# Attention over a 64-word vocabulary: exponentials of four of sixteen heads with the maximum as a per-partition bias and the sums from the same instruction

## Chip, cores and metric

One core of a Trainium2 chip runs the whole program. The metric is the device time of one execution in microseconds (us), as the median of several runs. Engines are TensorE (PE, matmuls; PEld is its weight load), VectorE (DVE), ScalarE (ACT), GpSimd (POOL) and SyncE (SP, which issues DMAs). All data are float32.

## The reference, cut to what matters

The program is a small language-model tower: token attention, a recurrent layer, and an expert layer. The change lies in the token attention. There are 32 sequences of 128 tokens from a vocabulary of 64 words, 16 heads of 16 dimensions:

```
emb = emb_W.T[input_seq] + emb_b
q, k, v = emb @ Wq.T + bq, emb @ Wk.T + bk, emb @ Wv.T + bv     # per head
scores = einsum('bqhd,bkhd->bhqk', q, k) / sqrt(d)
probs = softmax(scores, axis=-1)
ctx = einsum('bhqk,bkhd->bqhd', probs, v)
y = ctx @ Wo.T + bo + emb            # then a normalisation over each sequence
```

A token's row depends only on its word and on how often each word occurs in its sequence. So the kernel computes, for each sequence, the 64 rows of its words and not 128 rows of tokens: the score of a query word and a key word, plus the logarithm of the key word's count in the sequence, goes into the softmax over 64 key words.

## The kernel before, in words

Two sequences lie on the 128 partitions at a time (64 query words each), which makes 16 pairs. `score` [128, 16 heads, 64 keys] is computed once; `logc` holds the logarithms of the counts, one row of 64 per pair. The function `token_attention` has a first block that makes these tables, and a second block, with the change in it, that goes over the pairs. The steps for one pair, with their lines, are:

- GpSimd `logits`, L401: logit = score + logc, 1024 elements a partition. It waits for the exponential of two pairs earlier (buffers are double).
- VectorE `softmax_input`: L430 takes the maximum of each head into `ps_top`, which lies in PSUM; L431 subtracts it from `logit` in place, 16 heads at once.
- ScalarE `exponential`, L476: one Exp over 1024 elements into `prob`.
- GpSimd `partial_sums`: L409 adds the two halves of each head's 64 probabilities (512 results), and L411 the halves of that (256 results), waiting for L409 by a semaphore.
- VectorE `denominators`: L438 sums the remaining 16 of each head, L439 takes the reciprocal.
- TensorE `transpose_prob`, L518: eight transposes into PSUM; ScalarE `copy_prob`, L482, copies them to SBUF; TensorE `context`, L526, multiplies by the values.
- ScalarE `repeat_inverse`, L488, TensorE `spread`, L536, and ScalarE `copy_spread`, L493, bring the reciprocals into the layout of the context.
- VectorE `normalise`, L446, multiplies both into `cx_t`; TensorE `project`, L544; VectorE `output`: L453 adds the embedding, L455 takes statistics, L456 copies six numbers a partition into `stats6`, SBUF to SBUF. ScalarE `keep_row`, L497, stores the row.

Each engine works through its own list in a fixed order. In the turn of pair n the order is:

```
POOL: logits(n), partial_sums(n-1)
DVE:  softmax_input(n), normalise(n-2), denominators(n-1), output(n-3)
ACT:  copy_prob(n-1), copy_spread(n-2), exponential(n), repeat_inverse(n-1), keep_row(n-3)
PE:   context(n-1), project(n-2), transpose_prob(n), spread(n-1)
```

The first four and the last three turns are written out with the missing pairs left out, and the twelve turns between run in a hardware loop of two turns each. The recurrence and the expert layer follow, each in blocks of its own, behind a barrier.

Of the kernel before, what the change touches and what calls it, by code (L numbers as in the profile page):

```python
# [13 lines left out]
F32 = mybir.dt.float32  # L14
I32 = mybir.dt.int32
ALU = mybir.AluOpType
ACT = mybir.ActivationFunctionType
AX = mybir.AxisListType

P = 128  # L20
B, T = 32, 128
E, C = 256, 64
H, D = 16, 16
# [11 lines left out]
START = 16  # L35


class Chain:
# [15 lines left out]
    def enter(self, i, per, first=0):  # L54

        self.base, self.k, self.i, self.per, self.first = self.base + self.k, 0, i, per, first
# [102 lines left out]
def token_attention(nc, a, m, sem, sb):  # L159
# [177 lines left out]
    with ExitStack() as ctx:  # L337
        def sbx(n, s):
            return ctx.enter_context(nc.sbuf_tensor(n, s, F32))
        logit = [sbx(f"logit{i}", [P, H, C]) for i in range(2)]  # L340
        prob = [sbx(f"prob{i}", [P, H * C]) for i in range(2)]
        prob_t = [sbx(f"prob_t{i}", [P, HP, P]) for i in range(2)]
        half = [sbx(f"half{i}", [P, H, C // 2]) for i in range(2)]
        quarter = [sbx(f"quarter{i}", [P, H, C // 4]) for i in range(2)]
        den = [sbx(f"den_h{i}", [P, H]) for i in range(2)]
        rden = [sbx(f"rden_h{i}", [P, H]) for i in range(2)]
        r_rep = [sbx(f"r_rep{i}", [P, H, D]) for i in range(2)]
# [4 lines left out]
        ps_t = ctx.enter_context(nc.psum_tensor("ps_t", [P, HP * P], F32))  # L352
        ps_c = [ctx.enter_context(nc.psum_tensor(f"ps_c{i}", [P, 512], F32)) for i in range(2)]
        ps_y = [ctx.enter_context(nc.psum_tensor(f"ps_y{i}", [P, 512], F32)) for i in range(2)]
        ps_top = ctx.enter_context(nc.psum_tensor("ps_top", [P, 512], F32))
        block = ctx.enter_context(nc.Block())

        def par(name):
            return [sem(f"{name}{i}") for i in range(2)]
        sc_ok, lg_ok, ex_ok, hf_ok, dn_ok, rd_ok, rr_ok, rs_mm, rs_ok = (  # L360
            par(n) for n in ("sc_ok", "lg_ok", "ex_ok", "hf_ok", "dn_ok", "rden_ok", "rr_ok", "rs_mm", "rs_ok"))
        pt_mm, pt_ok, cx_mm, cx_ok, y_mm, y_ok, h_ok = (
            par(n) for n in ("pt_mm", "pt_ok", "cx_mm", "cx_ok", "y_mm", "y_ok", "h_ok"))
        TURNS = PAIRS // 2

        def pairs(t, s, live):

            for back in range(4):
                yield (t - (back + 1 - s) // 2, (s + back) % 2) if back in live else None

        def turns(work, enter=None):

            for n in range(4):
                work(*pairs(n // 2, n % 2, range(0, n + 1)))
            yield
            for n in range(1, 4):
                work(*pairs(TURNS + (n - 1) // 2, (n - 1) % 2, range(n, 4)))

        def run(eng, work, enter=None, leave=None):

            prefix = turns(work)
            next(prefix)
            with eng.Fori(2, TURNS) as t:
                if enter:
                    enter(t)
                for s in range(2):
                    work(*pairs(t, s, range(4)))
            if leave:
                leave()
            for _ in prefix:  # L390
                pass
# [5 lines left out]
        @block.gpsimd  # L397
        def _(pool):
            def logits(i, s):
                pool.wait_ge(ex_ok[s], START + i)  # L400
                nc.gpsimd.tensor_tensor(logit[s][:], score[:],  # L401
                                        logc[:, bass.ds(2 * i + s, 1)].broadcast_to([P, H, C]), ALU.add)\
                    .then_inc(sc_ok[s], 1)

            def partial_sums(i, s):
                p = prob[s][:].rearrange("p (h c) -> p h c", c=C)
                pool.wait_ge(ex_ok[s], START + i + 1)
                pool.wait_ge(rd_ok[s], START + i)
                nc.gpsimd.tensor_tensor(half[s][:], p[:, :, 0:C // 2], p[:, :, C // 2:], ALU.add).then_inc(hf_ok[s], 1)  # L409
                pool.wait_ge(hf_ok[s], START + i + 1)  # L410
                nc.gpsimd.tensor_tensor(quarter[s][:], half[s][:, :, 0:C // 4], half[s][:, :, C // 4:], ALU.add)\  # L411
                    .then_inc(dn_ok[s], 1)

            def work(p0, p1, p2, p3):
                if p0:
                    logits(*p0)
                if p1:
                    partial_sums(*p1)

            run(nc.gpsimd, work)  # L420

        @block.vector
        def _(dve):
            ch = Chain(dve, sem("v_chain1"))

            def softmax_input(i, s):

                top = ps_top[:, s * H:(s + 1) * H]
                dve.wait_ge(sc_ok[s], START + i + 1)
                ch.link(nc.vector.reduce_max(top, logit[s][:], AX.X))  # L430
                nc.vector.tensor_tensor(logit[s][:], logit[s][:], top.unsqueeze(2).broadcast_to([P, H, C]),  # L431
                                        ALU.subtract).then_inc(lg_ok[s], 1)

            def denominators(i, s):

                dve.wait_ge(dn_ok[s], START + i + 1)
                dve.wait_ge(rr_ok[s], START + i)
                ch.link(nc.vector.reduce_sum(den[s][:], quarter[s][:], AX.X))  # L438
                nc.vector.reciprocal(rden[s][:], den[s][:]).then_inc(rd_ok[s], 1)  # L439

            def normalise(i, s):

                dve.wait_ge(cx_mm[s], START + i + 1)
                dve.wait_ge(rs_ok[s], START + i + 1)
                dve.wait_ge(y_mm[s], START + i)
                nc.vector.tensor_tensor(cx_t[s][:].rearrange("p k c -> p (k c)"), ps_c[s][:, 0:E],  # L446
                                        r_sp[s][:].rearrange("p k c -> p (k c)"), ALU.mult).then_inc(cx_ok[s], 1)

            def output(i, s):

                dve.wait_ge(y_mm[s], START + i + 1)
                dve.wait_ge(h_ok[s], START + i)
                nc.vector.tensor_tensor(yrow[s][:], ps_y[s][:, 0:E], base[:], ALU.add).then_inc(y_ok[s], 1)  # L453
                dve.wait_ge(y_ok[s], START + i + 1)
                ch.link(nc.vector.bn_stats(bn[s][:], yrow[s][:]))  # L455
                nc.vector.tensor_copy(stats6[:, bass.ds(2 * i + s, 1)], bn[s][:].unsqueeze(1))  # L456

            def work(p0, p1, p2, p3):
                if p0:
                    softmax_input(*p0)  # L460
                if p2:
                    normalise(*p2)
                if p1:
                    denominators(*p1)
                if p3:
                    output(*p3)

            run(nc.vector, work, lambda t: ch.enter(t, 6, 2), lambda: ch.leave(TURNS))

        @block.scalar  # L470
        def _(act):
            def exponential(i, s):
                act.wait_ge(lg_ok[s], START + i + 1)
                act.wait_ge(pt_mm[s], START + i)
                act.wait_ge(hf_ok[s], START + i)
                nc.scalar.activation(prob[s][:], logit[s][:].rearrange("p h c -> p (h c)"),  # L476
                                     ACT.Exp).then_inc(ex_ok[s], 1)

            def copy_prob(i, s):
                act.wait_ge(pt_mm[s], START + i + 1)  # L480
                act.wait_ge(cx_mm[s], START + i)
                nc.scalar.copy(prob_t[s][:].rearrange("p g c -> p (g c)"), ps_t[:]).then_inc(pt_ok[s], 1)  # L482

            def repeat_inverse(i, s):

                act.wait_ge(rd_ok[s], START + i + 1)
                act.wait_ge(rs_mm[s], START + i)
                nc.scalar.copy(r_rep[s][:], rden[s][:].unsqueeze(2).broadcast_to([P, H, D])).then_inc(rr_ok[s], 1)  # L488

            def copy_spread(i, s):  # L490
                act.wait_ge(rs_mm[s], START + i + 1)
                act.wait_ge(cx_ok[s], START + i)
                nc.scalar.copy(r_sp[s][:].rearrange("p k c -> p (k c)"), ps_c[s][:, E:2 * E]).then_inc(rs_ok[s], 1)  # L493

            def keep_row(i, s):
                act.wait_ge(y_ok[s], START + i + 1)
                nc.scalar.copy(h_tab[:, bass.ds(2 * i + s, 1)], yrow[s][:].unsqueeze(1)).then_inc(h_ok[s], 1)  # L497

            def work(p0, p1, p2, p3):
                if p1:  # L500
                    copy_prob(*p1)
                if p2:
                    copy_spread(*p2)
                if p0:
                    exponential(*p0)
                if p1:
                    repeat_inverse(*p1)
                if p3:
                    keep_row(*p3)

            run(nc.scalar, work)
# [1220 lines left out]
```

## Time and profile before

| | us |
|---|---|
| median of 3 runs | 904.01 |
| lowest and highest | 898.59, 905.11 |
| the profiled execution, device time | 905.7 |
| its span, first to last instruction | 904.0 |
| TensorE clock granted, mean, as a share of full | 0.902 |
| the block of the 16 pairs, within the span | about 30.5 to 119 |

The page gives, over the whole span, TensorE busy 719.5 us (80%), VectorE 615.3 (68%), ScalarE 355.3 (39%) and GpSimd 452.9 (50%). These shares mix stages that have different limits, so that the block of the 16 pairs has to be read by itself. A timeline row gives the start, the length and the idle time before an instruction. Lines of the kernel are given as L401, and so on. Instructions on one engine overlap a little in these rows: the next may start up to 0.1 us before the one ahead has ended.

### The profile page before, as it was taken

How to read it: one execution, taken by the hardware profiler on the slowest of the kernel's cores; microseconds unless marked ns; L12 is line 12 of the kernel's file. 1: busy time of each engine (PE TensorE's matmuls, PEld its weight loads, DVE VectorE, ACT ScalarE, POOL GpSimd, SP SyncE). 2: the span in 40 equal slices, each digit the busy share in tenths (PEclk: the TensorE clock that was granted, in tenths of full speed). 3: DMA queues.
4: the chain of work that ended last, by engine and by line, in shares of the span. 5: the costliest groups of instructions: out<-in, count | busy, mean ns of one | idle time of the engine just before them, and what ended most of it. 6: DMA issues, size and time to landing. Idle time of an engine off the chain costs nothing. (4 is left out here: it accounts for less than half of the span.)

```text
span 904.0 us, 20491 instructions
## 1 busy us (share of the span) xinstructions
PE 719.5 (80%) x7708; PEld 484.6 (54%) x7708; DVE 615.3 (68%) x913; ACT 355.3 (39%) x562; POOL 452.9 (50%) x257
## 2 busy tenths in 40 slices
PE   3566758895999999999999999986899679867644
PEld 2354534443777777777777777755676423322221
DVE  1688847777899999999999999983676501100004
ACT  2456523442544545455454545433456221010100
POOL 1588700000799999999999999991221000000000
PEclk9789869987899999999999999996999879877875
DMA  4000010000001010000000000004900579999936
GB/s 107 1 1 0 0 49 0 0 0 14 6 12 34 13 36 12 12 12 12 12 9 9 12 12 12 14 13 152 348 26 2 208 282 410 417 416 416 402 121 209
DMA packets 48892, 86.34 MB, mean 96 GB/s; under 512 B 5233, under 2 KB 32433, under 8 KB 48849
## 3 DMA queue, kind: packets, MB, share of 16 engines
q1 hardware_dynamic: 43248, 81.23, 24.3%
q10 hardware_dynamic: 5600, 4.53, 1.6%
q8 instruction: 28, 0.46, 0.2%
q14 instruction: 16, 0.12, 0.0%
HBM read 76.31 MB, written 9.44 MB: 95 GB/s over the span
## 5 line engine op out<-in xcount | busy, mean ns | idle before, releaser
L859 POOL TENSOR_TENSOR read<-state,q_pos 128x1024 f32<-128x1024 f32 x128 | 300.4, 2366 | 28.0 <-DVE state L968 21.7
L968 DVE TENSOR_TENSOR_SCAN state<-fac,ps_up 128x1024 f32<-128x1024 f32 x128 | 290.0, 2277 | 13.0 <-ACT fac L903 12.6
L903 ACT ACTIVATE fac<-ps_xf 128x1016 f32<-128x1016 f32 x128 | 130.3, 1018 | 174.7 <-PE ps_xf L998 163.7
L998 PE MATMUL ps_xf<-hot,xtab 64*128 64x128 f32 x2048 | 149.0, 285 | 9.9 <-ACT fac L903 9.9
L998 PEld LDWEIGHTS ps_xf<-hot,xtab 64*128 64x128 f32 x2048 | 126.3, 189 | 56.4 <-ACT fac L903 45.2
L998 PE MATMUL ps_up<-hot,utab 64*128 64x128 f32 x2048 | 140.7, 277 | 18.2 <-DVE state L968 16.8
L998 PEld LDWEIGHTS ps_up<-hot,utab 64*128 64x128 f32 x2048 | 127.1, 190 | 23.7 <-issue 16.0
L868 POOL TENSOR_TENSOR utab<-tab 128x1024 f32 (+1 forms) x32 | 64.5, 2014 | 106.5 <-SPq L85 106.5
L1041 PE MATMUL ps_o<-read,sel 128*32 128x256 f32 x1024 | 82.7, 395 | 3.7 <-POOL read L859 3.7
L1582 DVE COPY h_t<-ps_ht 128x512 f32<-128x512 f32 x16 | 10.4, 687 | 78.1 <-PE ps_ht L1610 78.1
L958 DVE TENSOR_TENSOR xtab<-tab,ps_k 128x1024 f32<-128x1024 f32 x64 | 59.5, 929 | 1.5 <-PE ps_k L990 1.5
L1622 PE MATMUL ps<-w_sb,h_t 128*32 128x256 f32 x512 | 37.6, 448 | 19.1 <-DMA w_sb<-in_L_ffn_w 19.1
L401 POOL TENSOR_TENSOR logit<-score,logc 128x1024 f32<-128x1024 f32 x16 | 37.8, 2362 | 24.7 <-SPq L85 24.7
L1600 PE MATMUL ps<-w_sb,mq 128*32 128x512 f32 x256 | 40.8, 781 | 6.3 <-DMA w_sb<-in_L_ffn_w 6.3
L753 PE MATMUL ps_qk<-w_all,x_t 128*128 128x512 f32 x64 | 35.6, 685 | 7.5 <-ACT x_t L700 7.5
L1584 DVE COPY eo<-ps 128x256 f32 x8 | 3.4, 425 | 56.0 <-PE ps L1622 56.0
L958 DVE TENSOR_TENSOR utab<-tab,ps_k 128x1024 f32<-128x1024 f32 x32 | 38.3, 1196 | 0.0
L1521 ACT COPY mq<-merged 128x256 f32 (+1 forms) x8 | 3.2, 404 | 88.4 <-PE ps L1622 87.7
L1622 PEld LDWEIGHTS ps<-w_sb,h_t 128*32 128x32 f32 x512 | 17.5, 124 | 36.8 <-issue 24.8
L1376 PE MATMUL pq_h<-w_out,y_t 128*128 128x256 f32 x128 | 31.1, 386 | 5.9 <-DVE y_t L1299 5.9
L920 ACT COPY xtab<-xtab 128x512 f32<-128x512 f32 x32 | 34.8, 1088 | 0.0
L1041 PEld LDWEIGHTS ps_o<-read,sel 128*32 128x32 f32 x1024 | 20.2, 108 | 23.8 <-POOL read L859 5.5
(203 smaller groups left out, 979.6 us busy)
## 6 DMA issues: line engine op xcount, KB each, us to landing
w_sb<-in_L_ffn_w SPq DMA_DIRECT2D x32, 2048.0 KB, 19.5
rec_out<-osb SPq DMA_DIRECT2D x128, 32.0 KB, 1.5
ao<-rec_out SPq DMA_DIRECT2D x8, 512.0 KB, 4.0
out_dram<-res ACTq DMA_DIRECT2D x8, 512.0 KB, 2.8
tok<-in_x SPq DMA_DIRECT2D x2, 512.0 KB, 7.6
exp_out<-eo SPq DMA_DIRECT2D x8, 128.0 KB
oq<-exp_out SPq DMA_DIRECT2D x2, 512.0 KB, 4.2
w_nat<-in_L_tok_Wq SPq DMA_DIRECT2D x1, 256.0 KB, 9.0
```

What stands on the lines that cost most here:

```text
L401: nc.gpsimd.tensor_tensor(logit[s][:], score[:], logc[:, bass.ds(2 * i + s, 1)].broadcast_to([P, H, C]), ALU.add)\
L753: last = nc.tensor.matmul(ps_qk[s][:], x1_t[s][:, k], w_all[:, k, 0:2 * E], start=k == 0, stop=k == KT - 1)
L859: nc.gpsimd.tensor_tensor(read[n % 2][:], state[n % 4][:].rearrange("p (b i t) -> p b i t", b=2, i=IB), q_pos[x.s][:, :, x.k].unsqueeze(2) ...
L868: nc.gpsimd.tensor_tensor(out, feat, k_feat.rearrange("p (h j) -> p h j", j=D).unsqueeze(1) .broadcast_to([P, D // 2, HB, D]), ALU.mult).t ...
L903: nc.scalar.activation(fac[n % 2][:].rearrange("p (n t) -> p n t", t=T)[:, :, 1:], ps_x[:].rearrange("p (n t) -> p n t", t=T)[:, :, 1:], A ...
L920: nc.scalar.copy(rows[:, D // 2:, :, 0:D // 2], rows[:, 0:D // 2, :, D // 2:].rearrange("p j h i -> p i h j")).then_inc(t_act, 1)
L958: nc.vector.tensor_tensor(out[:, :, :, cols], feat[:, :, :, cols], ps_k[:, x.k * P:(x.k + 1) * P].rearrange("p (h j) -> p h j", j=D)[:, :, ...
L968: nc.vector.tensor_tensor_scan(state[n % 4][:], fac[n % 2][:], ps_u[n % 2][:], 0.0, ALU.mult, ALU.add)\
L998: last = nc.tensor.matmul(dst[:, b * 512 + col * T:b * 512 + (col + 1) * T], stationary[rows], pos[rows], start=True, stop=True)
L1041: last = nc.tensor.matmul(ps_o[32 * ii:32 * ii + 32, x.k * 256:(x.k + 1) * 256], sel[:, x.block], read[n % 2][:, :, ii], start=x.block == ...
L1600: last = nc.tensor.matmul(ps_1[s][j * B:(j + 1) * B, cols], mq[s][:, k, j], w1[s][:, j, k, cols], start=False, stop=k == KT - 1, skip_grou ...
L1622: last = nc.tensor.matmul(ps_2[s][j * B:(j + 1) * B, 0:E], h_t[:, n, j * B:(j + 1) * B], w2[s][:, j, n], start=False, stop=n == HT - 1, sk ...
```

## The change

For the last four heads VectorE no longer subtracts the maximum. The reduction (with `negate`) writes the negated maxima of all sixteen heads into a tile `low` in SBUF, and has a semaphore `mx_ok` of its own. VectorE then adds `low` to the logits of the first twelve heads. For each of the last four heads ScalarE runs an Exp of 64 elements with that head's column of `low` as the bias and with `accum_out`, which puts the sum into the head's column of `den`. Then it takes the Exp of the first twelve heads, 768 elements, as before. GpSimd's partial sums and VectorE's last sum are over twelve heads. The PSUM tile `ps_top` is gone. ScalarE's four small instructions wait for `mx_ok`, and for the transposes and the reciprocals of two pairs earlier; the large one waits for `lg_ok` and `hf_ok`.

```diff
--- before.py
+++ after.py
@@ -340,8 +340,10 @@
         logit = [sbx(f"logit{i}", [P, H, C]) for i in range(2)]
         prob = [sbx(f"prob{i}", [P, H * C]) for i in range(2)]
         prob_t = [sbx(f"prob_t{i}", [P, HP, P]) for i in range(2)]
-        half = [sbx(f"half{i}", [P, H, C // 2]) for i in range(2)]
-        quarter = [sbx(f"quarter{i}", [P, H, C // 4]) for i in range(2)]
+        HV = H - 4
+        half = [sbx(f"half{i}", [P, HV, C // 2]) for i in range(2)]
+        quarter = [sbx(f"quarter{i}", [P, HV, C // 4]) for i in range(2)]
+        low = [sbx(f"low{i}", [P, H]) for i in range(2)]
         den = [sbx(f"den_h{i}", [P, H]) for i in range(2)]
         rden = [sbx(f"rden_h{i}", [P, H]) for i in range(2)]
         r_rep = [sbx(f"r_rep{i}", [P, H, D]) for i in range(2)]
@@ -352,13 +354,12 @@
         ps_t = ctx.enter_context(nc.psum_tensor("ps_t", [P, HP * P], F32))
         ps_c = [ctx.enter_context(nc.psum_tensor(f"ps_c{i}", [P, 512], F32)) for i in range(2)]
         ps_y = [ctx.enter_context(nc.psum_tensor(f"ps_y{i}", [P, 512], F32)) for i in range(2)]
-        ps_top = ctx.enter_context(nc.psum_tensor("ps_top", [P, 512], F32))
         block = ctx.enter_context(nc.Block())
 
         def par(name):
             return [sem(f"{name}{i}") for i in range(2)]
-        sc_ok, lg_ok, ex_ok, hf_ok, dn_ok, rd_ok, rr_ok, rs_mm, rs_ok = (
-            par(n) for n in ("sc_ok", "lg_ok", "ex_ok", "hf_ok", "dn_ok", "rden_ok", "rr_ok", "rs_mm", "rs_ok"))
+        sc_ok, mx_ok, lg_ok, ex_ok, hf_ok, dn_ok, rd_ok, rr_ok, rs_mm, rs_ok = (
+            par(n) for n in ("sc_ok", "mx_ok", "lg_ok", "ex_ok", "hf_ok", "dn_ok", "rden_ok", "rr_ok", "rs_mm", "rs_ok"))
         pt_mm, pt_ok, cx_mm, cx_ok, y_mm, y_ok, h_ok = (
             par(n) for n in ("pt_mm", "pt_ok", "cx_mm", "cx_ok", "y_mm", "y_ok", "h_ok"))
         TURNS = PAIRS // 2
@@ -403,7 +404,7 @@
                     .then_inc(sc_ok[s], 1)
 
             def partial_sums(i, s):
-                p = prob[s][:].rearrange("p (h c) -> p h c", c=C)
+                p = prob[s][:].rearrange("p (h c) -> p h c", c=C)[:, 0:HV]
                 pool.wait_ge(ex_ok[s], START + i + 1)
                 pool.wait_ge(rd_ok[s], START + i)
                 nc.gpsimd.tensor_tensor(half[s][:], p[:, :, 0:C // 2], p[:, :, C // 2:], ALU.add).then_inc(hf_ok[s], 1)
@@ -425,17 +426,18 @@
 
             def softmax_input(i, s):
 
-                top = ps_top[:, s * H:(s + 1) * H]
                 dve.wait_ge(sc_ok[s], START + i + 1)
-                ch.link(nc.vector.reduce_max(top, logit[s][:], AX.X))
-                nc.vector.tensor_tensor(logit[s][:], logit[s][:], top.unsqueeze(2).broadcast_to([P, H, C]),
-                                        ALU.subtract).then_inc(lg_ok[s], 1)
+                nc.vector.tensor_reduce(low[s][:], logit[s][:], AX.X, ALU.max, negate=True).then_inc(mx_ok[s], 1)
+                dve.wait_ge(mx_ok[s], START + i + 1)
+                nc.vector.tensor_tensor(logit[s][:, 0:HV], logit[s][:, 0:HV],
+                                        low[s][:, 0:HV].unsqueeze(2).broadcast_to([P, HV, C]),
+                                        ALU.add).then_inc(lg_ok[s], 1)
 
             def denominators(i, s):
 
                 dve.wait_ge(dn_ok[s], START + i + 1)
                 dve.wait_ge(rr_ok[s], START + i)
-                ch.link(nc.vector.reduce_sum(den[s][:], quarter[s][:], AX.X))
+                ch.link(nc.vector.reduce_sum(den[s][:, 0:HV], quarter[s][:], AX.X))
                 nc.vector.reciprocal(rden[s][:], den[s][:]).then_inc(rd_ok[s], 1)
 
             def normalise(i, s):
@@ -465,15 +467,20 @@
                 if p3:
                     output(*p3)
 
-            run(nc.vector, work, lambda t: ch.enter(t, 6, 2), lambda: ch.leave(TURNS))
+            run(nc.vector, work, lambda t: ch.enter(t, 4, 2), lambda: ch.leave(TURNS))
 
         @block.scalar
         def _(act):
             def exponential(i, s):
+                act.wait_ge(mx_ok[s], START + i + 1)
+                act.wait_ge(pt_mm[s], START + i)
+                act.wait_ge(rd_ok[s], START + i)
+                for h in range(HV, H):
+                    nc.scalar.activation(prob[s][:, h * C:(h + 1) * C], logit[s][:, h], ACT.Exp, bias=low[s][:, h:h + 1],
+                                         scale=1.0, accum_out=den[s][:, h:h + 1])
                 act.wait_ge(lg_ok[s], START + i + 1)
-                act.wait_ge(pt_mm[s], START + i)
                 act.wait_ge(hf_ok[s], START + i)
-                nc.scalar.activation(prob[s][:], logit[s][:].rearrange("p h c -> p (h c)"),
+                nc.scalar.activation(prob[s][:, 0:HV * C], logit[s][:, 0:HV].rearrange("p h c -> p (h c)"),
                                      ACT.Exp).then_inc(ex_ok[s], 1)
 
             def copy_prob(i, s):

```

## Rows read from the trace of the kernel before

**Rows 1.** Windows view: busy us of PE, PEld, DVE, ACT, POOL; clock; DMA share, GB/s.

```profile
...
30.00:48.00 18.00, 9.75 (x64) 7.57 (x64) 11.38 (x13) 7.27 (x10) 15.91 (x11) 0.62 0.00 1
63.00:68.00 5.00, 3.97 (x26) 3.19 (x14) 4.71 (x9) 1.75 (x3) 4.49 (x4) 0.66 0.00 0
30.00:119.40 89.40, 57.10 (x480) 43.54 (x480) 72.60 (x128) 49.87 (x82) 69.29 (x48) 0.85 0.00 0
```

**Rows 2.** Groups by line and shape, 40 to 110 us: total, mean ns, idle before.

```profile
...
L401 POOL TENSOR_TENSOR logit<-score,logc 128x1024 f32<-128x1024 f32 x14 | 33.1, 2365 | 0.0
...
L409 POOL TENSOR_TENSOR half<-prob 128x512 f32<-128x512 f32 x14 | 17.9, 1277 | 7.6 <-ACT prob L476 7.6
...
L431 DVE TENSOR_TENSOR logit<-logit,ps_top 128x1024 f32<-128x1024 f32 x14 | 17.1, 1221 | 0.5
L430 DVE TENSOR_REDUCE ps_top<-logit 128x16 f32<-128x1024 f32 x14 | 17.1, 1219 | 2.2 <-POOL logit L401 1.9
...
L411 POOL TENSOR_TENSOR quarter<-half 128x256 f32<-128x256 f32 x14 | 10.3, 736 | 1.1
...
L438 DVE TENSOR_REDUCE den_h<-quarter 128x16 f32<-128x256 f32 x13 | 5.3, 408 | 0.0
```

**Rows 3.** Timeline, a pair at the full clock: start us, length us, instruction, idle before.

```profile
...
88.27 1.22 DVE L431 TENSOR_TENSOR logit<-logit,ps_top 128x1024 f32<-128x1024 f32 x1
...
89.52 1.06 ACT L476 ACTIVATE prob<-logit 128x1024 f32<-128x1024 f32 x1 [1.17 <-DVE logit L431]
...
89.88 1.13 PE L544 MATMUL ps_y<-w_t,cx_t 128*128 128x256 f32 x4 [1.10 <-DVE cx_t L446]
...
90.74 1.28 POOL L409 TENSOR_TENSOR half<-prob 128x512 f32<-128x512 f32 x1 [0.52 <-ACT prob L476]
...
90.84 1.04 PE L518 MATMUL ps_t<-ident,prob 128*128 128x128 f32 x8
...
91.34 0.70 DVE L456 COPY stats<-bn 128x6 f32 x1 [0.16 <-DVE bn L455]
...
91.96 1.22 DVE L430 TENSOR_REDUCE ps_top<-logit 128x16 f32<-128x1024 f32 x1
91.99 1.01 ACT L482 COPY prob_t<-ps_t 128x1024 f32<-128x1024 f32 x1 [0.72 <-PE ps_t L518]
```

**Rows 4.** Timeline, a pair at the lower clock.

```profile
...
64.29 2.01 PE L544 MATMUL ps_y<-w_t,cx_t 128*128 128x256 f32 x4 [1.03 <-DVE cx_t L446]
...
66.10 1.87 PE L518 MATMUL ps_t<-ident,prob 128*128 128x128 f32 x8
...
68.01 1.01 ACT L482 COPY prob_t<-ps_t 128x1024 f32<-128x1024 f32 x1 [2.32 <-PE ps_t L518]
...
69.18 1.07 ACT L476 ACTIVATE prob<-logit 128x1024 f32<-128x1024 f32 x1
```

**Rows 5.** Timeline, the copy of L456 after GpSimd's last instruction.

```profile
...
115.70 0.17 DVE L456 COPY stats<-bn 128x6 f32<-128x6 f32 x1
```

**Rows 6.** Instructions of L1222, min/median/max ns, in the expert gate's softmax.

```profile
...
L1222 ACT ACTIVATE pr<-lg_q,nmx x8: 401/403/403, 648.2 to 723.5; 128x128 f32<-128x128 f32 x8
L1222 ACT ACTIVATION_READ_ACCUMULATOR pr<-lg_q,nmx x8: 186/188/191, 648.5 to 723.8; 128x1 f32 x8
```

**Rows 7.** VectorE with two SBUF operands, 24 to 29 us.

```profile
...
L289 DVE TENSOR_TENSOR log_diag<-ident,cnt 128x1024 f32<-128x1024 f32 x1 | 1.2, 1224 | 0.0
...
L294 DVE TENSOR_TENSOR v_pair<-v_tab,row_half 128x256 f32<-128x256 f32 x1 | 0.4, 426 | 0.0
```

**Rows 8.** Timeline of GpSimd, 29 to 34 us.

```profile
...
30.48 4.64 POOL L401 TENSOR_TENSOR logit<-score,logc 128x1024 f32<-128x1024 f32 x2 [24.69 <-SPq L85]
```

**Rows 9.** Timeline of ScalarE: its exponentials of pairs 0, 3 and 15.

```profile
...
35.37 1.06 ACT L476 ACTIVATE prob<-logit 128x1024 f32<-128x1024 f32 x1 [2.79 <-DVE logit L431]
...
49.15 1.07 ACT L476 ACTIVATE prob<-logit 128x1024 f32<-128x1024 f32 x1
...
109.78 1.07 ACT L476 ACTIVATE prob<-logit 128x1024 f32<-128x1024 f32 x1
```


## Prediction, on record before the change was run

> **What bounds the kernel now.** I read the windows of the block first, then its groups by shape, then the timeline of one pair at each level of the clock. In the windows the reader is to see that no DMA runs in these 89.4 us, that VectorE is busy 72.6 and GpSimd 69.3 of them, and that TensorE's clock falls from full to 0.66 in single pairs and to 0.62 in the filling [rows 1]. The block is a tenth of the span, and nothing behind its barrier reads what the change touches except through its end, so whatever the change does is a shift of that end. The exponentials of pairs 3 and 15 start at 49.15 and 109.78 [rows 9]: 60.63 us for twelve pairs, 5.05 each. That is the number to move.
>
> Two rings share that period. At the full clock VectorE's own list is the ring: the subtraction starts at 88.27, and the next can start when the maximum of 91.96 has ended, at about 93.2, so 4.94 us [rows 3]. ScalarE waits 1.17 us for VectorE there. At the lower clock it is TensorE and ScalarE: the projection takes 2.01 instead of 1.13 us and the transposes 1.87 instead of 1.04, the copy of the probabilities starts at 68.01, and the exponential follows at 69.18 with no wait for VectorE [rows 3, 4].
>
> One row in VectorE's list is more than its work. The copy of six numbers, L456, takes 0.17 us once GpSimd has finished [rows 5], but 0.70 us beside GpSimd's L409: it ends at 92.04, L409 at 92.02 [rows 3]. It is held until GpSimd's instruction ends, then needs 0.02 us, and VectorE's next maximum waits behind it. The subtraction L431 keeps its 1.22 us beside the 2.37 us additions of GpSimd; its second operand is in PSUM [rows 2].
>
> **The change part by part.**
>
> *VectorE.* An element costs (1221-426)/768 = 1.035 ns, with L431 for the 1024 and a 256-element addition in SBUF for the other end [rows 2, 7]. So 768 elements take 0.95 us, 0.27 less. The last sum, L438 with 408 ns for 256, loses 64 elements: 0.07 less. The maximum into SBUF instead of PSUM I cost at nothing (a VectorE addition of 1024 takes 1224 ns into SBUF and L430 1219 into PSUM [rows 2, 7]; bound 0 to 0.05). Its new semaphore wait replaces the one of the chain. In all 0.34 us less in a list of 4.9.
>
> *GpSimd.* (1277-736)/256 = 2.11 ns an element [rows 2]: L409 falls by 0.27 to 1.01 us, L411 by 0.14 to 0.60. The additions L401 stay at 2.37. GpSimd's list falls from 4.38 to 3.98 us a pair.
>
> *ScalarE.* The large exponential falls from 1.06 to about 0.85 us. Four small ones are added. The nearest row is L1222, bias, sum and 128 elements: 403 ns, with a second instruction of 188 ns that reads the accumulator [rows 6]. With 64 fewer elements at 0.83 ns that is 0.35 plus 0.19; neighbours overlap by up to 0.09, once or twice, so 0.35 to 0.44 each after the first overlap. I take 0.40, so 1.6 us for the four, bounds 1.4 and 1.8. Net +1.4 us of ScalarE a pair. At the full clock ScalarE has 1.17 us of wait ahead of the exponential [rows 3] and the small ones need only the maximum, so most of it hides there: they run while VectorE subtracts. At the lower clock there is no wait, and all 1.4 us lies on the ring. Queued behind the four are the large exponential, the repeat of the inverses and the row's copy; who waits is TensorE's transposes and GpSimd's L409. (The Trainium skill, "ScalarE: Activation LUTs", section "What ACT_TABLE_LOAD costs", gives 280 ns plus 0.833 ns an element with a bias pointer: an estimate of 0.33 us for 64 elements, and for 128 it gives 387 where the trace has 403; with it the four would take about 1.7 us.)
>
> ScalarE's ring after the change: 1.17 from the copy's start to the exponential's [rows 4], 1.6, 0.85 less 0.1, 0.1 to TensorE, the transposes 1.04 or 1.87 [rows 3, 4], and 0.1 to the next copy (90.84+1.04 to 91.99 [rows 3]): 4.8 us at the full clock, 5.65 at the lower.
>
> *The place of the maxima.* The subtraction now has both operands in SBUF. No row shows such an instruction beside a running GpSimd instruction: the two of rows 7 ran before 29 us, and GpSimd sat idle until 30.48 [rows 7, 8]. The nearest rows point both ways: L431 with a PSUM operand is not held, the copy L456 is. So the bounds are no wait at all and the whole of an L401, 2.37 us. The sum L438, which reads one SBUF tile and writes another, keeps its 408 ns and is free too [rows 2], so it is not enough that nothing is in PSUM. I take it, as the likelier half, that two SBUF operands are held like the copy; the instruction then pays only its streaming, 0.80 us, after the release. (The Trainium skill, "SBUF — State Buffer", section "Who interferes with whom", says so outright: a VectorE instruction with two SBUF inputs contends with a GpSimd instruction that reads SBUF, and the second to issue is blocked until the first has finished. It speaks against this change. The trace agrees as to the copy; as to two inputs no row shows it. By it rival 2 below falls away.)
>
> **What the period becomes.** If held, VectorE's subtraction and GpSimd's three instructions share one way. Where the subtraction goes in ahead of the next L401, the ring is 2.37 + 1.01 + 0.08 + 0.60 + 0.80 and 0.02 for the copy = 4.9 us, about ScalarE's 4.8. From pair 3 on, with four of the twelve pairs at the lower clock as now (the window from 63 us, and three like it from 73, 94 and 104 [rows 1]): 8 x 4.9 + 4 x 5.65 = 61.8, against 60.63: +1.2 us. The filling, at 0.62 of the clock, goes from 13.78 us between exponentials 0 and 3 [rows 9] to three rounds of 5.65 less the part for which the clock is up again, about 16.3: +2.5. The first subtraction, which ended just ahead of the exponential of 35.37 and so began at about 34.1 [rows 9], would be held by the second L401, which ends at 35.12 [rows 8]: +0.6. Sum +4.3 us on a span of 904.0 and a device time of 905.7, so a profile of 910.0; from the median 904.0 it is 908.3. Bounds of the four exponentials move it by 1.5 to 2.5: 904 to 912.
>
> **The rivals.**
>
> 1. *Held, and GpSimd goes first (slower).* When L411 ends, L401 is queued right behind it, and the subtraction waits too. No row tells who is let through. If it is GpSimd, or if VectorE comes after L401 has begun, the subtraction sits out all of L401, and the exponential, L409 and L411 come behind it one after another: exponential 0.89, 0.16 to GpSimd (90.58 to 90.74 [rows 3]), 1.01, 0.08, 0.60, 2.37, then 0.80 = 5.9 us. VectorE's next maximum only starts when the copy is released at the end of L409, and so comes too late again: the state keeps itself up. It decides where the maximum ends later than L411, that is 0.7 us after L409. Twelve pairs give 70.8: +10.2, with the filling +13.3, so 917; lower-clock pairs may add 0.9 each, up to 921. For it: the copy's 0.70 us. Against: VectorE would have been waiting longer.
>
> 2. *Not held.* VectorE's ring falls to 4.6 us and ScalarE's of 4.8 and 5.65 sets the period: 61.0 for twelve, +0.4, with +2.5 in the filling: 907. For it: L431 and L438 run undisturbed beside GpSimd [rows 2]. It gives nearly the same time as the forecast; the rows of the subtraction tell them apart.
>
> 3. *The small exponentials all hide.* ScalarE is busy 49.9 of 89.4 us [rows 1]. If lower-clock pairs get rare, 12 x 4.7 = 56.4: -4.2, about 900. Against: the ring above, which has no slack.
>
> **How the numbers follow.** Forecast (held, subtraction ahead of L401) 0.38, rival 1 0.36, rival 2 0.18, rival 3 0.05, anything else 0.03. The likeliest time is 908.3, its own range 904 to 912. For 8 in 10 the range has to take in most of rival 1: 903 to 919. One per cent, 9 us, is about what a measurement of this kernel can tell. Over it lies nearly all of rival 1 and a little of the forecast's upper end: slower 0.39; faster 0.02; the rest 0.59.
>
> **What the profile would show.** Subtraction rows at 0.95 us beside GpSimd: not held. Rows of 1 to 3 us that end some 0.02 to 0.8 us behind the end of a GpSimd instruction: held; if they end behind L401, rival 1, and GpSimd then waits for ScalarE before each L409. Four exponentials of 0.35 us with four reads of 0.19. ScalarE's wait for VectorE gone at the full clock, TensorE's transposes waiting for `prob`. L409 near 1.01 and L411 near 0.60. Everything behind the block shifted as a whole. The prediction is wrong if the later blocks change length, if the small exponentials cost over 0.5 us each, or if the clock's level changes over the block.

## The result and the profile after

| | before | after |
|---|---|---|
| median, 17 runs each | 902.32 us | 914.26 us |
| lowest and highest | 898.01, 905.53 | 905.63, 918.46 |
| ratio, 95% interval | | 1.0124 [1.0105, 1.0143] |
| profiled execution: device time, span | 905.7, 904.0 | 913.17, 911.4 |
| block of the 16 pairs, first L401 (L402) to the next block's table load | 30.48 to 119.37 | 28.53 to 129.46 |

The change makes the kernel 1.24% slower, 11.9 us by the medians. In the profiled executions the block lasts 88.9 us before and 100.9 after, 12.0 more. The rest of the program took 4.6 us less in the profiled execution of after (1.95 ahead of the block, the others behind it), which is why the span grew by 7.4 only; runs of one kernel differ by as much.

From here on the lines are those of the changed kernel: L402 is the large addition (L401 before), L410 and L412 the partial sums (L409, L411), L430 the maximum, L432 the subtraction (L431), L458 the copy of the six numbers (L456), L479 the small exponentials and L483 the large one (L476). The windows view of after, with the columns of [rows 1]:

```profile
...
104.00:109.00 5.00, 4.33 (x22) 3.44 (x26) 4.71 (x7) 2.48 (x6) 3.90 (x3) 0.50 0.00 0
28.50:129.00 100.50, 63.12 (x480) 46.91 (x480) 82.63 (x127) 66.62 (x209) 65.84 (x48) 0.78 0.00 0
```

VectorE is busier by 10 us than in [rows 1], though it was given less to do, GpSimd has 3.5 us less, and TensorE has the same 480 matmuls at a mean clock of 0.78 instead of 0.85. The groups by shape, from 40 to 125 us, with total, mean ns and idle before, answer to [rows 2], which go from 40 to 110:

```profile
...
L402 POOL TENSOR_TENSOR logit<-score,logc 128x1024 f32<-128x1024 f32 x13 | 31.3, 2410 | 0.0
L432 DVE TENSOR_TENSOR logit<-logit,low 128x768 f32<-128x768 f32 x14 | 27.5, 1966 | 0.5
...
L479 ACT ACTIVATE prob<-logit,low 128x64 f32<-128x64 f32 x56 | 18.8, 345 | 0.0
...
L410 POOL TENSOR_TENSOR half<-prob 128x384 f32<-128x384 f32 x15 | 15.0, 1000 | 25.8 <-ACT prob L483 25.8
...
L412 POOL TENSOR_TENSOR quarter<-half 128x192 f32<-128x192 f32 x15 | 11.0, 731 | 1.2
L479 ACT ACTIVATION_READ_ACCUMULATOR prob<-logit,low 128x1 f32 x56 | 10.9, 195 | 0.0
```

The subtraction of 768 elements has a mean of 1966 ns where 1024 elements took 1221 [rows 2]. GpSimd's first sum costs 1.00 us, as worked out, but GpSimd sat idle ahead of it, waiting for the exponential, for 25.8 us in 15 sums, 1.7 each; in [rows 2] it was 7.6 in 14, 0.5 each. The small exponentials cost 345 and 195 ns. The next timeline shows how such a wait begins; each row is start, length, instruction, idle before:

```profile
...
56.23 1.00 POOL L410 TENSOR_TENSOR half<-prob 128x384 f32<-128x384 f32 x1
56.36 0.89 DVE L458 COPY stats<-bn 128x6 f32 x1 [0.20 <-DVE bn L457]
...
57.17 1.21 DVE L430 TENSOR_REDUCE low<-logit 128x16 f32<-128x1024 f32 x1
57.31 0.60 POOL L412 TENSOR_TENSOR quarter<-half 128x192 f32<-128x192 f32 x1
57.86 2.35 POOL L402 TENSOR_TENSOR logit<-score,logc 128x1024 f32<-128x1024 f32 x1
...
58.41 2.62 DVE L432 TENSOR_TENSOR logit<-logit,low 128x768 f32<-128x768 f32 x1
58.41 0.35 ACT L479 ACTIVATE prob<-logit,low 128x64 f32<-128x64 f32 x1
...
61.06 0.84 ACT L483 ACTIVATE prob<-logit 128x768 f32<-128x768 f32 x1 [1.22 <-DVE logit L432]
...
62.06 1.00 POOL L410 TENSOR_TENSOR half<-prob 128x384 f32<-128x384 f32 x1 [1.85 <-ACT prob L483]
```

GpSimd's first sum L410 starts at 56.23. The copy L458 is asked for at 56.36 and ends at 57.25, 0.02 us after L410. So the maximum starts only at 57.17 and the subtraction is asked for at 58.41, 0.55 us after the large addition L402 has begun. It runs to 61.03, which is 0.82 us after L402 has ended at 60.21: it was held for as long as the addition ran and then streamed its 768 elements. Everything behind it is late: the large exponential starts at 61.06, and GpSimd does nothing from 60.21 to 62.06. Nine subtractions in a row (pairs 5 to 13) take 2.23 to 2.63 us in this manner. The tenth escapes:

```profile
...
110.20 0.83 ACT L483 ACTIVATE prob<-logit 128x768 f32<-128x768 f32 x1
...
111.03 0.17 DVE L458 COPY stats<-bn 128x6 f32 x1 [0.16 <-DVE bn L457]
...
111.50 1.22 DVE L430 TENSOR_REDUCE low<-logit 128x16 f32<-128x1024 f32 x1 [0.30 <-issue]
...
112.26 0.59 POOL L412 TENSOR_TENSOR quarter<-half 128x192 f32<-128x192 f32 x1
112.75 0.96 DVE L432 TENSOR_TENSOR logit<-logit,low 128x768 f32<-128x768 f32 x1
112.82 3.10 POOL L402 TENSOR_TENSOR logit<-score,logc 128x1024 f32<-128x1024 f32 x1
```

Here the exponential is late for another reason (TensorE's lower clock, 0.50 in the window from 104 to 109 us above), GpSimd starts L410 late at 111.19, and the copy has slipped in ahead of it. The subtraction is asked for at 112.75, 0.07 us before the large addition is. It takes 0.96 us, and now the addition is the one that is held: 3.10 us instead of 2.35.

The starts of the large exponential give one pair of numbers for each kernel, the filling (pair 0 to 3) and twelve pairs (3 to 15), as in [rows 9]. They stand in this table for all runs, each from its profiled execution, beside the median and the ratio to the kernel before on the same chip, which had medians of 902.32 to 902.80 us:

| kernel | filling | twelve pairs | median us | ratio, 95% interval |
|---|---|---|---|---|
| before | 13.78 | 60.63 | | |
| after | 16.45 | 70.18 | 914.26 | 1.0124 [1.0105, 1.0143] |
| place_only | 14.57 | 65.15 | 909.62 | 1.0074 [1.0049, 1.0100] |
| place_stats_psum | 14.58 | 65.13 | 909.44 | 1.0089 [1.0057, 1.0121] |
| two_places | 15.70 | 55.68 | 900.83 | 0.9979 [0.9957, 1.0001] |
| after_stats_psum | 16.43 | 55.85 | 900.75 | 0.9957 [0.9928, 0.9985], without two of the six runs (see there) |
| before_stats_psum | 13.89 | 57.82 | 899.36 | 0.9961 [0.9941, 0.9982] |
| ordered | 16.42 | 60.41 | 904.21 | 1.0017 [0.9998, 1.0035] |
| two_stats_psum | 16.43 | 55.67 | 900.60 | 0.9980 [0.9958, 1.0001] |
| two_stats_hv2 | 14.55 | 56.52 | 901.19 | 0.9981 [0.9962, 1.0000] |
| two_hv8 | 19.16 | 70.01 | 919.05 | 1.0176 [1.0143, 1.0209] |
| no_accum | 15.38 | 60.01 | 902.60 | 1.0001 [0.9984, 1.0018] |

### The profile page after: what moved, and what is told of

The parts are those of the page before. It is cut to its first block and busy times, and to the rows that moved or that the text cites. A ratio compares the mean times of both kernels' runs of the same rounds, so it can differ in the third digit from the quotient of the medians.

```text
span 911.4 us, 20625 instructions
## 1 busy us (share of the span) xinstructions
PE 720.2 (79%) x7708; PEld 485.1 (53%) x7708; DVE 625.5 (69%) x913; ACT 371.8 (41%) x690; POOL 449.5 (49%) x257
## 5 line engine op out<-in xcount | busy, mean ns | idle before, releaser
L402 POOL TENSOR_TENSOR logit<-score,logc 128x1024 f32<-128x1024 f32 x16 | 38.3, 2397 | 22.8 <-SPq L85 22.8
L760 PE MATMUL ps_qk<-w_all,x_t 128*128 128x512 f32 x64 | 33.1, 643 | 9.2 <-ACT x_t L707 9.2
L551 PE MATMUL ps_y<-w_t,cx_t 128*128 128x256 f32 x64 | 23.8, 508 | 13.8 <-DVE cx_t L448 13.6
```

What stands on the lines that cost most here:

```text
L402: nc.gpsimd.tensor_tensor(logit[s][:], score[:], logc[:, bass.ds(2 * i + s, 1)].broadcast_to([P, H, C]), ALU.add)\
L760: last = nc.tensor.matmul(ps_qk[s][:], x1_t[s][:, k], w_all[:, k, 0:2 * E], start=k == 0, stop=k == KT - 1)
```

## The experiments

The theory after the result was: the subtraction's second operand in SBUF makes it and GpSimd's instructions exclude each other; whichever is asked for first goes first; the held copy brings VectorE late, and from then on each pair loses the overlap. The rival was that the small exponentials on ScalarE cost the time.

**place_only.** The kernel before with only the place of the maxima changed, sixteen heads and no small exponentials.

```diff
-                top = ps_top[:, s * H:(s + 1) * H]
+                top = low[s][:]
```

> The kernel before with one edit: the maxima go to a tile in SBUF instead of PSUM, sixteen heads as before, no small exponentials. Theory (the place of the maxima costs the time, the subtraction is held while GpSimd runs): subtraction rows of 2.5 to 3 us that end about 1.07 us after a GpSimd addition of 2.37; a ring of 1.06 + 0.16 + 1.28 + 0.08 + 0.74 + 2.33 + 1.07 = 6.7 us against 5.05, so up to 20 us slower than the kernel before, at least 8 if the subtraction often gets in ahead. Rival (the small exponentials cost the time): within 2 us of the kernel before.

Measured: 0.74% slower, with a period of 5.42 to 5.44 us in every pair from pair 2 on. Its timeline (L409, L411 and L401 are GpSimd's three, as before):

```profile
...
68.57 1.27 POOL L409 TENSOR_TENSOR half<-prob 128x512 f32<-128x512 f32 x1
68.65 1.22 DVE L430 TENSOR_REDUCE low<-logit 128x16 f32<-128x1024 f32 x1
...
69.91 1.23 DVE L431 TENSOR_TENSOR logit<-logit,low 128x1024 f32<-128x1024 f32 x1
69.92 1.81 POOL L411 TENSOR_TENSOR quarter<-half 128x256 f32<-128x256 f32 x1
...
71.69 2.36 POOL L401 TENSOR_TENSOR logit<-score,logc 128x1024 f32<-128x1024 f32 x1
...
74.01 1.27 POOL L409 TENSOR_TENSOR half<-prob 128x512 f32<-128x512 f32 x1
```

The subtraction is asked for at 69.91, L411 at 69.92. The subtraction takes its plain 1.23 us, and L411 takes 1.81 instead of 0.74: this time GpSimd is held. So the place alone costs 0.7% with no small exponential in the program, which the rival doesn't give. The size of 20 us was wrong, since from pair 2 on VectorE asks first each time, if only by 0.01 to 0.03 us; the milder figure of at least 8 was still above the 6.8 us measured. The period is the sum of what now excludes each other: 2.36 + 1.27 + 1.81 less overlaps of a few hundredths.

**place_stats_psum.** The same, and the statistics tile in PSUM.

```diff
-        bn = [sbx(f"bn{i}", [P, 6]) for i in range(2)]
+        bn = [ps_bn[:, 64 + 8 * i:64 + 8 * i + 6] for i in range(2)]
```

> The kernel before with the maxima in SBUF and the statistics tile in PSUM. Theory (in place_only the shared way itself is the ring: addition 2.36, first sum 1.27, subtraction 1.07, second sum 0.74, 5.43 us, with the subtraction already ahead of the addition): freeing the copy brings nothing, 5 to 8 us slower than the kernel before. Rival (the held copy costs in this kernel too): within 3 us of the kernel before.

Measured: 65.13 us for twelve pairs against 65.15, and 0.89% slower than before. The copy falls from 0.69 to 0.17 us and the period stays. Where VectorE asks first anyway, the held copy costs nothing that can be measured.

**two_places.** The changed kernel, its maxima in two reductions: those for ScalarE's bias in SBUF, those for the subtraction in PSUM.

```diff
-                nc.vector.tensor_reduce(low[s][:], logit[s][:], ...).then_inc(mx_ok[s], 1)
-                dve.wait_ge(mx_ok[s], START + i + 1)
+                nc.vector.tensor_reduce(low[s][:, HV:H], logit[s][:, HV:H], ...).then_inc(mx_ok[s], 1)
+                top = ps_top[:, s * H:s * H + HV]
+                ch.link(nc.vector.tensor_reduce(top, logit[s][:, 0:HV], ...))
...
-                                        low[s][:, 0:HV].unsqueeze(2).broadcast_to([P, HV, C]),
+                                        top.unsqueeze(2).broadcast_to([P, HV, C]),
```

> The changed kernel with the maxima in two reductions: those of the last four heads into SBUF for ScalarE, those of the twelve others into PSUM for the subtraction; the small exponentials with their sums stay. Theory (place): subtraction rows of 0.95 us throughout, GpSimd's first partial sum no longer late by 1.8 us, time between 1 us faster and 4 us slower than the kernel before. Rival (the small exponentials): still 8 to 12 us slower.

Measured: 900.83, a ratio of 0.9979, so by the two ratios 1.4% below the changed kernel with all of ScalarE's new work kept. The rival falls. One pair of its timeline (L434 is the subtraction, L481 the small exponentials, L485 the large one, L527 the transposes, L491 the copy of the probabilities):

```profile
...
65.06 1.01 ACT L491 COPY prob_t<-ps_t 128x1024 f32<-128x1024 f32 x1 [0.61 <-PE ps_t L527]
...
65.58 2.37 POOL L403 TENSOR_TENSOR logit<-score,logc 128x1024 f32<-128x1024 f32 x1
...
66.19 0.95 DVE L434 TENSOR_TENSOR logit<-logit,ps_top 128x768 f32<-128x768 f32 x1
66.23 0.36 ACT L481 ACTIVATE prob<-logit,low 128x64 f32<-128x64 f32 x1
...
67.56 0.83 ACT L485 ACTIVATE prob<-logit 128x768 f32<-128x768 f32 x1
...
68.50 1.05 PE L527 MATMUL ps_t<-ident,prob 128*128 128x128 f32 x8
...
69.66 1.01 ACT L491 COPY prob_t<-ps_t 128x1024 f32<-128x1024 f32 x1 [0.66 <-PE ps_t L527]
```

The subtraction is asked for at 66.19, 0.61 us after the large addition (L403 here) has begun, as late as in the changed kernel. With its second operand in PSUM it takes 0.95 us and isn't held. From the copy at 65.06 to the next at 69.66 there are 4.6 us: copies 1.17, four small exponentials 1.33, the large one 0.83, about 0.1 to TensorE, transposes 1.05 and 0.1 back. ScalarE and TensorE are now the ring, and the subtraction has slack.

**after_stats_psum.** The changed kernel with the statistics tile in PSUM, by the same edit as place_stats_psum. The subtraction keeps both operands in SBUF.

> The changed kernel with the statistics tile of six numbers in PSUM, so that VectorE's small copy is not held by GpSimd's partial sum. Theory (the late state keeps itself up only because the copy is held, and whoever asks first goes first): the maximum starts up to 0.7 us earlier, the subtraction asks before the large addition starts, and about half of the loss goes: 4 to 7 us slower than the kernel before. Rival (the subtraction is held however early it asks, or GpSimd has precedence): 10 to 13 us slower, as the changed kernel.

Measured: six runs of 897.88, 897.97, 899.51, 901.98, 914.12 and 916.13 us. The ratio of 0.9957 is that of the first four. I had expected half of the loss to go; in four runs all of it went, and a little more, and in two the kernel took as long as the changed one (905.63 to 918.46). The timeline of the 899.51 us execution (L403 is the large addition, L433 the subtraction, L459 the copy):

```profile
...
67.90 0.17 DVE L459 COPY stats<-ps_bn 128x6 f32 x1 [0.18 <-DVE ps_bn L458]
68.13 1.00 POOL L411 TENSOR_TENSOR half<-prob 128x384 f32<-128x384 f32 x1
68.20 1.22 DVE L431 TENSOR_REDUCE low<-logit 128x16 f32<-128x1024 f32 x1
...
69.20 0.60 POOL L413 TENSOR_TENSOR quarter<-half 128x192 f32<-128x192 f32 x1
69.45 1.16 DVE L433 TENSOR_TENSOR logit<-logit,low 128x768 f32<-128x768 f32 x1
...
69.76 3.08 POOL L403 TENSOR_TENSOR logit<-score,logc 128x1024 f32<-128x1024 f32 x1
```

The copy takes 0.17 us, the maximum starts at 68.20, and the subtraction is asked for at 69.45, after the second sum L413 began and before the addition. It is held until L413 ends at 69.80 only. The addition, asked for at 69.76, waits for it and takes 3.08 us. In the profiled execution the late state is never entered, but the margin is thin: in ten pairs of the loop the subtraction is asked for only 0.16 to 0.31 us ahead of the addition. No trace was taken of the two long runs. Their mean clocks of 0.892 and 0.894 are near that of the changed kernel's profiled execution, 0.895, and below the 0.902 to 0.912 of the other four, so the late state is the likely reason, but that isn't shown.

**ordered.** The changed kernel with one wait more on GpSimd, and the copy still held.

```diff
                 pool.wait_ge(ex_ok[s], START + i)
+                pool.wait_ge(lg_ok[1 - s], START + i + s)
                 nc.gpsimd.tensor_tensor(logit[s][:], score[:],
```

> The changed kernel with one wait more: GpSimd starts the large addition for a pair only when VectorE has finished the subtraction of the pair ahead. Statistics tile in SBUF, so the small copy is still held. Theory (what costs is that the addition starts ahead of the subtraction): no subtraction longer than about 1.8 us, none that ends behind the large addition, period 4.6 to 4.9 us, 1 us faster to 3 us slower than the kernel before. Rival (the held copy costs by itself, or the lost overlap costs as much): 6 to 12 us slower, like the changed kernel.

Measured: 1.0017 [0.9998, 1.0035], twelve pairs in 60.41 us against 70.18. Making GpSimd wait a little takes 9.8 us out of the loop:

```profile
...
70.79 0.87 DVE L459 COPY stats<-bn 128x6 f32 x1 [0.17 <-DVE bn L458]
...
71.66 1.22 DVE L431 TENSOR_REDUCE low<-logit 128x16 f32<-128x1024 f32 x1
...
72.92 1.16 DVE L433 TENSOR_TENSOR logit<-logit,low 128x768 f32<-128x768 f32 x1
...
74.26 0.83 ACT L484 ACTIVATE prob<-logit 128x768 f32<-128x768 f32 x1
74.26 2.37 POOL L403 TENSOR_TENSOR logit<-score,logc 128x1024 f32<-128x1024 f32 x1 [1.00 <-DVE logit L433]
```

The copy is still held, for 0.87 us, and yet the subtraction takes 1.16 us and the addition, released by it, 2.37. All twelve runs lie between 900.37 and 906.11 us. So the order is what cost the time. In the profiled execution of the changed kernel the held copy led into the bad order; the two long runs of after_stats_psum leave open whether something else can too.

**before_stats_psum.** The kernel before with the statistics tile in PSUM.

> The kernel before with the statistics tile in PSUM. Theory (VectorE's list is the ring at the full clock, and the held copy is 0.4 to 0.5 us of it): copy rows of 0.17 us, the ring 4.94 falls to about 4.5 in eight of twelve pairs, 2 to 4 us faster than the kernel before. Rival (TensorE and ScalarE take over at once): within 1 us.

Measured: 0.39% faster than the kernel before, 899.36 us, with twelve pairs in 57.82 us. It is the version with the lowest median here and lies clear of the two given kernels; its interval overlaps those of two_places, two_stats_psum and two_stats_hv2, so that no order among these is shown.

**two_stats_psum.** two_places with that edit too.

> The kernel with two reductions, and the statistics tile in PSUM as well. Theory (with the subtraction free, ScalarE and TensorE are the ring, 4.6 us at the full clock: copy of the probabilities to the next copy): freeing the held copy of VectorE brings nothing more, within 1.5 us of two_places, so about 2 us faster than the kernel before. Rival (the held copy still sets the period): 4 to 6 us faster than the kernel before.

Measured: 55.67 us for twelve pairs against 55.68 in two_places, medians 900.60 and 900.83. With ScalarE and TensorE as the ring, freeing the copy brings nothing, as expected.

**two_hv8.** two_places with eight heads by small exponentials: `HV = H - 8`.

> The kernel with two reductions, with eight heads by small exponentials instead of four, so their cost doubled. Theory (ring of ScalarE, 4 x 0.333 - 0.21 = 1.12 us more in each of some 15 periods): period 5.7 us, 14 to 18 us slower than two_places. Rival (they hide in ScalarE's idle time of some 0.6 us a pair): at most 8 us slower than two_places.

Measured: 18.2 us above two_places by the medians (taken on two chips), at the upper end of the 14 to 18 expected. ScalarE's timeline, one pair:

```profile
...
79.77 1.01 ACT L491 COPY prob_t<-ps_t 128x1024 f32<-128x1024 f32 x1 [0.66 <-PE ps_t L527]
...
80.94 0.36 ACT L481 ACTIVATE prob<-logit,low 128x64 f32<-128x64 f32 x1
81.19 0.20 ACT L481 ACTIVATION_READ_ACCUMULATOR prob<-logit,low 128x1 f32 x1
81.29 0.34 ACT L481 ACTIVATE prob<-logit,low 128x64 f32<-128x64 f32 x1
...
83.61 0.62 ACT L485 ACTIVATE prob<-logit 128x512 f32<-128x512 f32 x1
...
85.41 1.01 ACT L491 COPY prob_t<-ps_t 128x1024 f32<-128x1024 f32 x1 [0.58 <-PE ps_t L527]
```

From copy to copy there are 5.64 us, 1.04 more than with four. A small exponential starts every 0.33 us (80.94, 81.29), and with eight there are 2.67 us of them between the copies and the large one. They don't hide.

**two_stats_hv2.** Two heads by small exponentials: `HV = H - 2`, otherwise as two_stats_psum.

> The same with two heads by small exponentials instead of four. Theory (ring of ScalarE): it loses 2 x 0.33 less 0.11, about 0.55 us a pair, and the ring passes to VectorE's list at about 4.45; 0.1 to 0.2 us a pair and the filling about 1 us shorter: 2 to 4 us faster than two_stats_psum at most. Rival (small exponentials hide in ScalarE's idle time): no difference from two_stats_psum.

Measured: 0.9981 against 0.9980. The filling is 1.9 us shorter and the twelve pairs 0.85 longer; I expected a gain of 2 to 4 us at most, and none can be measured. Three pairs of 5.2 to 5.6 us are in its loop and one in that of two_places; why they are rarer there wasn't tried.

**no_accum.** two_places, but the small exponentials give no sum, and the partial sums are over sixteen heads again.

```diff
-                                         scale=1.0, accum_out=den[s][:, h:h + 1])
+                                         scale=1.0)
```

> The kernel with two reductions; the four small exponentials keep the bias but give no sum, and the partial sums are over all sixteen heads again. Theory: no reads of the accumulator, small exponentials 0.24 to 0.26 us apart instead of 0.333, ScalarE's ring 0.3 to 0.4 shorter, but VectorE's ring of about 4.6 to 4.7 takes over with the first partial sum at 1.28 again: within 2 us of two_places either way. Rival (the reads are the main cost of the small exponentials): 4 us or more faster than two_places.

Measured: 902.60, 1.8 us above two_places, with intervals that still touch. The groups by shape from 40 to 110 us:

```profile
...
L411 POOL TENSOR_TENSOR half<-prob 128x512 f32<-128x512 f32 x15 | 19.1, 1275 | 11.5 <-ACT prob L484 11.4
...
L481 ACT ACTIVATE prob<-logit,low 128x64 f32<-128x64 f32 x56 | 14.9, 347 | 0.0
...
L460 DVE COPY stats<-bn 128x6 f32 x12 | 7.8, 649 | 2.1 <-DVE bn L459 2.1
```

The reads of the accumulator are gone, and no time is gained. The first sum is back at 1275 ns, where two_places has 1005, but the copy has a mean of 649 ns against 590, so the hold is nearly the same. Eight of the twelve periods are 4.5 to 4.6 us, as in two_places, and four are 5.7 to 6.2, where two_places has one of 5.4; the mean clock over the twelve was 0.89 against 0.97. So the reads are not the main cost of the small exponentials, as was expected; why nothing is gained without them isn't shown.

## Why the prediction came out as it did

The time lay in the range, and the loss was the one that rival 1 describes, but the likeliest case named was another. Step by step:

- *What bounds the block.* The copy was read rightly: it was held by GpSimd in before, and moving its source to PSUM (before_stats_psum) took it to 0.17 us, the twelve pairs from 60.63 to 57.82 us and the kernel 0.39% down. That VectorE's list was the ring at the full clock is borne out by this.
- *Elements.* Subtraction 0.95 us: it measured 0.96 undisturbed. First sum 1.01: 1.00. Second 0.60: 0.60. Large exponential 0.85: 0.84. Last sum 0.07 less: 339 ns against 408.
- *Small exponentials.* 1.6 us for four, bounds 1.4 and 1.8: they measured 1.33, a start every 0.33 us, below the lower bound. The read starts 0.1 us before the exponential ends and the next exponential 0.1 us before the read ends; I had counted the overlap between one and two times. ScalarE's ring, put at 4.8, was 4.6. (From the 280 ns plus 0.833 ns an element of the Trainium skill, "ScalarE: Activation LUTs", section "What ACT_TABLE_LOAD costs", the estimate for one was 0.33 us; the rows show 345 ns.) The read took 195 ns.
- *The place of the maxima.* Taken as held, with 0.80 us of streaming after the release: held, with 0.82. (The Trainium skill, "SBUF — State Buffer", section "Who interferes with whom", has a VectorE instruction with two SBUF inputs contend with a GpSimd instruction that reads SBUF. The trace agrees: the subtraction took 2.62 us beside the addition with both inputs in SBUF and 0.95 us in two_places with one in PSUM.)
- *Who goes first.* "Where the subtraction goes in ahead of the next L401" was the failed step. I took the question to be who is let through when both wait, and gave VectorE slightly the better chance, 0.38 against 0.36. On that it was right: whoever was asked for first went first in each case shown, 0.01 us apart in place_only and 0.07 in the escape, and in after_stats_psum the subtraction that waited on the second sum went in ahead of the addition. But VectorE did not ask first. From pair 5 to pair 13 the subtraction asked 0.54 to 0.93 us too late. I had written down the condition myself, a maximum that ends more than 0.7 us after L409, and did not put the numbers in: a copy that is held until L409 ends puts the end of the maximum 1.2 us behind it. The trace of before shows this order directly, in two pairs in a row (88.27 in [rows 3], with its addition at 87.85, and this one):

```profile
...
92.79 2.37 POOL L401 TENSOR_TENSOR logit<-score,logc 128x1024 f32<-128x1024 f32 x1
...
93.21 1.22 DVE L431 TENSOR_TENSOR logit<-logit,ps_top 128x1024 f32<-128x1024 f32 x1
```

  The subtraction asks 0.42 us after the addition has begun, which costs nothing there, with an operand in PSUM. The change makes L411 0.14 us shorter, and the addition that much earlier against the copy's release: an estimate of 0.56 us late, where the first held one was 0.55 us late. By that estimate rival 1 was the case to expect wherever L409 holds the copy.
- *Does the late state keep itself up?* It did for nine pairs, but less by the held copy than rival 1 says: among these the copy mostly takes 0.27 to 0.32 us. That is a hold of 0.10 to 0.15 us, where the next subtraction asked 0.55 to 0.93 too late: VectorE's own list after a late subtraction is long enough. In this execution the copy's hold is the way in (56.36) and not the whole of what keeps it there. That is read from the rows; no trace has the late state with the copy free, though two runs of after_stats_psum took as long as if they had been in it.
- *The sizes.* Filling +2.5 plus 0.6 for the first subtraction: +2.67 from exponential to exponential, and the first exponential started 5.49 us after the first addition against 4.89, the 0.6 that was put on the first subtraction. No part of the filling can be put down to the place: two_stats_psum, with the subtraction's maxima in PSUM, has 16.43 against 16.45. Two_places has 15.70, at a clock of 0.61 against 0.50 in two_stats_psum. Twelve pairs: rival 1 gave 70.8 us, measured 70.18. That is nearer than it deserved: it took twelve periods of 5.9, and the trace has nine late ones with a mean of 6.12, three of them 6.5 to 6.8, and three others with a mean of 5.02. Rival 1 as a whole gave 917, that is +13.3; measured +11.9.
- *Rivals 2 and 3.* Not held is refuted by the rows. That the small exponentials hide is refuted by two_hv8.
- *The sign that came true.* The prediction called itself wrong if the clock's level changed over the block. It did, from a mean of 0.85 to 0.78 (before and after, whole block), and the three long ones of the nine late periods go with it: their clocks were 0.50, 0.74 and 0.50, with transposes of 1.91 to 1.92 us instead of 1.04. The blocks behind were 2.7 us shorter in the profiled execution, within what runs of one kernel differ by.
- *What was missed on the other side.* With the order right in the trace of after_stats_psum, the loop is shorter than that of before, 55.85 against 60.63 us, not longer by the 1.2 forecast; in ordered, where GpSimd waits for it, it is 60.41. Part of that is the ring of 4.6. The rest may go with the clock: the granted share over those twelve pairs was 0.89 before, 0.81 after and 0.97 in two_places. Which of the two causes the other wasn't settled.

## What to carry to other kernels

Moving a small operand from PSUM to SBUF can cost more than the work that a change adds or takes away (place_only, 6.8 us): look at which VectorE instructions have all their operands in SBUF and what GpSimd does beside them, and read the ends, since a held row ends just behind the other engine's row. When two engines exclude each other, the order in which they ask is the quantity to predict; work out the time of each request, from the trace of the kernel before if it has both instructions, before asking who wins a tie, and force the order with one semaphore wait where it matters: here that gave twelve runs within 6 us, where freeing the copy gave four short runs and two long ones. A held instruction that is nearly free by itself, such as a copy of six numbers, can set that order for everything behind it.

## What was unexpected of the hardware

- A GpSimd addition is held by VectorE just as VectorE is by GpSimd: 3.08 us for one of 2.36, and 1.81 for one of 0.74. They were asked for 0.85 and 1.22 us before the VectorE instruction ended, and grew by 0.72 and 1.07 us.
- The reduction from SBUF into SBUF was never held (a mean of 1215 ns, also beside GpSimd's sums and additions), nor was the last sum, 339 ns.
- Adding a wait to GpSimd made the changed kernel 10 us faster (ordered, 904.21 against 914.26 us).
